# Value products on 16-bit operands in a kernel of two expert layers and one attention

## What is computed

```python
x = x + 0.5 * ffn(layernorm(x))
x = x + attention(layernorm(x))
x = x + 0.5 * ffn(layernorm(x))

def attention(x):                      # per sequence and head
    q, k, v = x @ (codes * repeat(scales, 32)) + b     # 256 -> 16 heads of 128
    attn = softmax(q @ k.T / sqrt(128))                # 512 x 512
    return (attn @ v) @ Wo + bo

def ffn(x):                            # router picks 2 of 16 experts
    return shared(x) + sum over the 2 of weight * expert(x)
```

## Time and profile before

| | us |
|---|---|
| median of 3 runs | 1041.41 (1041.18 to 1042.96) |
| the profiled execution | 1044.5 |
| its span, first to last instruction | 1042.7 |

### The profile page before, as it was taken

How to read it: one execution, slowest core, us unless ns; L and a number is a source line. 1 busy time by engine, 2 the same in 40 slices (tenths; PEclk the granted TensorE clock), 3 DMA queues, 4 the chain that set the end, 5 groups by cost and what they waited for, 6 DMA issues and landing times. The chain is left out here.

```text
span 1042.7 us, 18753 instructions
## 1 busy us (share of the span) xinstructions
PE 973.6 (93%) x5314; PEld 839.2 (80%) x5314; DVE 799.0 (77%) x1682; ACT 676.0 (65%) x1485; POOL 625.7 (60%) x916
## 2 busy tenths in 40 slices
PE   5669999899999999999999999999999999888996
PEld 4559987677888888888888888888888887668995
DVE  7777567889887787777877777787878888567766
ACT  4635644767687677677777776777776776325662
POOL 1740448776346768577788577687745456861155
PEclk9779999999999999999999999999999999789999
DMA  8867652775545764877768878767765447997755
GB/s 306 315 249 242 209 182 71 157 157 109 99 82 127 150 134 90 173 197 162 184 131 187 213 192 177 193 145 153 192 132 101 82 81 172 259 387 251 233 170 177
DMA packets 329891, 183.07 MB, mean 176 GB/s; under 512 B 273344, under 2 KB 314944, under 8 KB 329152
## 3 DMA queue, kind: packets, MB, share of 16 engines
q1 hardware_dynamic: 323056, 155.66, 60.5%
q0 software_dynamic: 6432, 20.98, 6.0%
q10 hardware_dynamic: 304, 5.24, 1.4%
HBM read 73.31 MB, written 46.92 MB: 115 GB/s over the span
## 5 line engine op out<-in xcount | busy, mean ns | idle before, releaser
L682 POOL CAST R<-turned 128x512 fp32r<-128x512 f16 x512 | 289.7, 615 | 212.9 <-DMA turned<-work 148.7
L1722 PE MATMUL bank<-R 128*128 128x512 f32 (+2 forms) x1056 | 388.4, 368 | 16.9 <-DVE R L1360 5.9
L1723 PE MATMUL bank<-R 128*128 128x512 f32 (+2 forms) x1056 | 377.8, 358 | 0.0
L1724 PE MATMUL bank<-R 128*128 128x512 f32 (+2 forms) x1056 | 377.3, 357 | 0.0
L1722 PEld LDWEIGHTS bank<-R 128*128 128x128 f32 x1056 | 202.7, 192 | 50.7 <-issue 9.8
L1724 PEld LDWEIGHTS bank<-R 128*128 128x128 f32 x1056 | 202.6, 192 | 28.3
L1723 PEld LDWEIGHTS bank<-R 128*128 128x128 f32 x1056 | 203.1, 192 | 27.0
L992 ACT ACTIVATE bank<-bank,soft 128x512 f32<-128x512 f32 x256 | 170.3, 667 | 70.5 <-DVE soft L1532 70.5
L1525 DVE SCALAR_TENSOR_TENSOR R<-bank,bias,R 128x512 fp32r<-128x512 f32 x192 | 143.8, 749 | 64.4 <-ACT R L1012 38.1
L1532 DVE TENSOR_REDUCE soft<-bank 128x1 f32<-128x512 f32 x256 | 168.6, 686 | 25.0 <-PE bank L1724 25.0
L1546 DVE SCALAR_TENSOR_TENSOR work<-bank,soft,work 128x512 f16<-128x512 f32 x256 | 185.3, 743 | 0.8 <-ACT work L1005 0.8
(11 more groups left out here) (164 smaller groups left out, 1379.1 us busy)
## 6 DMA issues: line engine op xcount, KB each, us to landing
work<-in_parts SPq DMA_DIRECT2D x64, 256.0 KB, 3.6
work<-in_ffn_w SPq DMA_DIRECT2D x34, 384.0 KB, 4.7
work<-xs_dram SPq DMA_DIRECT2D x96, 128.0 KB, 2.4
y_tiles<-work SPq DMA_DIRECT2D x48, 256.0 KB, 2.9
w_dram<-work SPq DMA_DIRECT2D x16, 768.0 KB, 4.5
R<-w_dram SPq DMA_DIRECT2D x16, 768.0 KB, 9.7
y_tiles<-in_empty ACTq DMA_DIRECT2D x2, 2176.0 KB
X<-in_x SPq DMA_DIRECT2D x4, 512.0 KB, 5.1
```

Source lines behind the costliest of these rows:

```text
L682: nc.gpsimd.tensor_copy(whole_into(m, l, kb), whole_block(m, u, l, kb)).then_inc(s["cast_pool"], 1)
L1722: nc.tensor.matmul(out, ah, bh, start=(i == 0 and first), stop=False)
L1723: nc.tensor.matmul(out, ah, bl, start=False, stop=False)
L1724: last = nc.tensor.matmul(out, al, bh, start=False, stop=(i == n - 1))
```

## The change

- The value products read the turned fp16 planes themselves, as four blocks of 128 columns each. Values V are fp16 planes, hi and lo. The casts and PT are gone; POOL only waits for the transposes. `pv` waits for both transposes ahead of its first product; `flip` and the shared weights' load wait for the value products (o) where they waited for casts.
- So that the values fit fp16, a group's value weights and bias are multiplied by a power of two, alpha. POOL squares the scaled weights of the four heads and adds them up (`squared`, `fold`), sends the 128 sums to HBM and reads them back on all partitions (`sums_out`, `sums_in`), adds them (`total`). DVE makes alpha and its inverse with five short integer operations (`scale_of`). POOL multiplies the weights with it (`halved`), `y_add` multiplies by the inverse. For groups 1 to 3 this is cut into six steps in as many units (`VALUE_STEPS`: from unit 4, 21 and 37, steps at +0, +1, +2, +3, +5, +6, DVE at +4); for group 0 it stands in the first feed-forward block.
- PT's room is put ahead of the value weights. Nine experts (0 to 8) are loaded during the attention (units 30, 31, 41, 45, 46, 52, 60, 61, 62), seven behind it.

```diff
+UP = 127 + 11 + 63
+DOWN = 254 - UP - 15
...
+FREE = 8192
...
+             nc.sbuf_tensor("V", [P, 2, 2, QB, HG * HD], F16) as m.V, \
...
-        m.PT = c.cut(2 * QB * S).rearrange("p (l b n) -> p l b n", l=2, b=QB)
...
+def value_start(g):
+    return 4 if g == 1 else HG * B * g - 11
...
+EXPERT_AT = {30: 0, 31: 1, 41: 2, 45: 3, 46: 4, 52: 5, 60: 6, 61: 7, 62: 8}
+VALUE_STEPS = {value_start(g) + step: (g, step) for g in range(1, NG) for step in (0, 1, 2, 3, 5, 6)}
+SCALED = {value_start(g) + 4: g for g in range(1, NG)}
...
-    return m.turned[u % 2][:, :, :, l, kb, :]
+    return m.turned[u % 2][:, :, :, l, kb, :].rearrange("p h q n -> p (h q) n")
...
-        wait(sp, s["cast_pool"], 8 * (u - 1))
+        wait(sp, s["o"], u - 1)
...
+    def fold(a, n):
+        while n > 1:
+            n //= 2
+            st.link(nc.gpsimd.tensor_tensor(a[:, 0:n], a[:, 0:n], a[:, n:2 * n], ALU.add))
...
+    def squared(g, i):
+        codes = m.raw[:, 0, part_of("v", g, i) % 4, :]
+        st.link(nc.gpsimd.tensor_tensor(one_head if i else squares, codes, codes, ALU.mult))
+        if i:
+            st.link(nc.gpsimd.tensor_tensor(squares, squares, one_head, ALU.add))
+    def sums_out(g):
+        fold(squares, KT * HD)
+        nc.gpsimd.dma_start(m.peak_dram[g:g + 1, :].rearrange("a p -> p a"), squares[:, 0:1])\
...
+    def scaled_bias(g):
+        pool.wait_ge(s["alpha"], 2 * g + 2)
...
+            st.link(nc.gpsimd.tensor_scalar(codes, codes, m.alpha[:, g, 0:1], None, ALU.mult))
...
-        wait(pool, s["o"], u)
-        for kb, l in ((0, 0), (0, 1), (1, 0), (1, 1), (2, 0), (2, 1), (3, 0), (3, 1)):
-            cast(u, l, kb)
...
+    def value_step(g, step):
+        if step < 2:
+            for i in (2 * step, 2 * step + 1):
+                scaled("v", g, i)
+            for i in (2 * step, 2 * step + 1):
+                squared(g, i)
+            if step == 1:
+                sums_out(g)
+        elif step == 2:
+            sums_in(g)
+        elif step == 3:
+            total(g)
+        else:
+            if step == 5:
+                scaled_bias(g)
+            for i in (2 * step - 10, 2 * step - 9):
+                halved("v", g, i)
...
+    def scale_of(g):
+        power, unit = m.peak[:, 1:2].bitcast(I32), 2.0 ** EXPONENT
+        dve.wait_ge(s["total"], g + 1)
...
-            ins = v_.scalar_tensor_tensor(out=x2, in0=bank[6 + i][:], scalar=1.0 / P_SCALE, in1=x2,
+            ins = v_.scalar_tensor_tensor(out=x2, in0=bank[6 + i][:], scalar=m.alpha[:, it // B, 1:2], in1=x2,
...
     def pv(u, kb):
-        pe.wait_ge(s["cast_pool"], 8 * u + 2 * kb + 2)
+        if kb == 0:
+            for half in range(2):
+                pe.wait_ge(m.flipped[half], 16 * (u + 1))
...
-        ph, pl = m.PT[:, 0, kb, :], m.PT[:, 1, kb, :]
-        nc.tensor.matmul(bank[1][:], vh, ph, start=(kb == 0), stop=False)
+        ph, pl = (whole_block(m, u, l, kb) for l in range(2))
+        out = bank[1][:].rearrange("p (a n) -> p a n", a=QB)
+        nc.tensor.matmul(out, vh, ph, start=(kb == 0), stop=False)
```

More of the change, by code:

```diff
@@ L198, in build @@
         m.y_tiles = nc.dram_tensor("y_tiles", (NR * P, D), F32, kind="Internal").ap()
+        m.peak_dram = nc.dram_tensor("peak_dram", (NG, P), F32, kind="Internal").ap()
         m.sh_dram = nc.dram_tensor("sh_dram", (P, 2 * W_SH), F32, kind="Internal").ap()
@@ L241, in build @@
         m.begin, m.shift, m.own, m.skipped = c.cut(SEG + 1), c.cut(SEG), c.cut(NE), c.cut(QB)
+        m.alpha = m.own[:, 0:2 * NG].rearrange("p (g n) -> p g n", g=NG)
         assert CH <= 4 * D
@@ L404, in weight_work @@
         for hh in range(HG):
-            at = 4 + hh // 2 if g == 1 else first - 8 + hh // 2
+            at = value_start(g) + hh // 2
             work.setdefault(at, []).append(("v", g, hh))
@@ L556, in sync_program @@
             empty_spare()
[L557 to L571, removed]
+        if u in EXPERT_AT:
+            e = EXPERT_AT[u]
+            sp.wait_ge(s["pre_out"], 16 * (e + 1))
+            if e >= 5:
+                sp.wait_ge(s["v"], 48 if e == 5 else 64)
+            if e == 8:
+                sp.wait_ge(s["o"], UNITS - 4)
+            expert(e)
+    sp.wait_ge(s["o"], UNITS - 1)
     sp.dma_start(m.sh_words, m.sh_dram).then_inc(s["sh_in"], 16)
@@ L574, in sync_program @@
     sp.wait_ge(s["q"], UNITS)
-    sp.wait_ge(s["y"], UNITS - 3)
-    expert(8)
     sp.wait_ge(s["s"], 4 * UNITS)
+    expert(15)
+    sp.wait_ge(s["y"], UNITS - 2)
+    expert(11)
+    sp.wait_ge(s["y"], UNITS - 1)
     expert(12)
-    sp.wait_ge(s["y"], UNITS - 2)
+    sp.wait_ge(s["o"], UNITS)
     expert(9)
[L581 to L584, removed]
     expert(10)
     sp.wait_ge(s["y"], UNITS)
-    expert(11)
+    expert(13)
+    expert(14)
     tile_loads(1)
@@ L708, in pool_program @@
         fetch(0, 0, j)
-    for value in values:
-        scaled(*value)
+        if j == 3:
+            scaled(*values[0])
+            scaled(*values[1])
+        if j == 4:
+            squared(0, 0)
+            squared(0, 1)
+        if j == 5:
+            scaled(*values[2])
+            scaled(*values[3])
+        if j == 6:
+            squared(0, 2)
+            squared(0, 3)
+        if j == 7:
+            sums_out(0)
+    sums_in(0)
+    total(0)
+    scaled_bias(0)
     pool.wait_ge(s["r_dn"], NPAIR)
@@ L759, in pool_program @@
     for t in range(1, UNITS + 1):
-        casts(t - 1)
-        for part in WEIGHTS_AT.get(t, ()):
-            weights(*part)
+        turned(t - 1)
+        if t in VALUE_STEPS:
+            value_step(*VALUE_STEPS[t])
+        for kind, g, hh in WEIGHTS_AT.get(t, ()):
+            if kind != "v":
+                weights(kind, g, hh)
         if t == 1:
```

48 lines of the change are left out of this document (36 added, 12 removed).

## The result

| | us |
|---|---|
| predicted | 1031.0 (1026 to 1039) |
| the changed kernel, median of 4 runs | 1053.24 (1050.48 to 1059.51) |
| the kernel before, beside it, median of 4 | 1041.30 (1040.94 to 1042.96) |
| ratio, 95% interval | 1.0121 (1.0094 to 1.0148) |
| the profiled execution, its span | 1059.51, 1057.7 |

A forecast was written before the change was run, and what follows sets the result against it. PE was taken to bound the attention, without a gap. Value products 7.6 plus late casts 3.0 made 10.6 us off the median 1041.4: 1030.8, rounded 1031.0, range 1026 to 1039 with (a) and (c), (b) left out.

The forecast's parts named there:

- What bounds the kernel, and reading it by starts: Attention, 290 to 860 us: PE busy 567.90 of 570.00 us, no gap by product starts, 10.98 us a head.
- Value products, 7.6 us: Attention's 768 value products: 16-bit operands save 10.8 ns each, counted for 708 of them, 7.6 us.
- lower bound: Value products: 8.3 ns saved each, 5.9 us, if a 16-bit product costs 5.0 ns over its columns.
- Rival (a): Value products: weight load already hidden, 13.3 ns belong to the product's issue; only the casts' 3.0 us left, 1038.4; chance 0.14.
- (b): Value products: four blocks of 128 each restart the stream, 39.8 ns more a product, 1069 us; chance 0.09.
- Late casts, 3.0 us: Attention: PE runs behind POOL's casts in five heads, 3.6 us; half of the second head's given back, 3.0 us.
- The new wait on both transposes, 0: Ahead of each head's first value product: planes ready at least 2.1 us before PE wants them, cost 0.
- POOL's new work in the attention, 0: Attention: worst head at most 11.8 us of POOL work, below the 14.7 allowed; cost 0, cover 2.9 us.
- Group 0's exchange: Ahead of the attention: no term; one clause, DVE's first operations fall where it is idle for 4.5 us.
- ScalarE, VectorE, the moved expert loads, the end: Attention and end: each costs 0; a moved load delays the next transposes about 1.6 us, which is covered.
- (c): Transposes late behind moved expert loads or POOL's long head: four places, 2 us each, 8 us, 1039; chance 0.11.
- (d): PE's clock: a fall to half clock after waits for DVE, spared or added, 2 us either way; no chance given.

The follow-up runs named there:

- constant_scale: Changed kernel with constant scale 64, put on where ScalarE and VectorE write the value planes; no search, exchange or multiply: ratio 0.9862 to the kernel before.
- before_again: The kernel before, unchanged, traced again on the second set's chip: one run, 1045.2 us, span 1043.4.
- work_only: Changed kernel with POOL's squares, folds and sums kept, but no write or read of the sums, total constant 512: ratio 0.9940 to the kernel before.
- scale_only: Changed kernel with one edit, scale put on at the values' planes instead of by POOL's multiply on the weights: ratio 1.0062 to the kernel before.
- at_eviction_b: The kernel of at_eviction measured again, on the third set's chip: ratio 0.9930 to the kernel before.
- at_eviction: Changed kernel with pre-splits of heads 22 and 38 later, group 0's exchange five fetches earlier, scale put on at value planes: ratio 0.9898.
- write_each_head: constant_scale plus a 0.5 KB write by POOL in each of heads 10 to 52: ratio 1.0466, 63 us over constant_scale.

## Why the prediction was wrong, point by point

Two sums from traces. What the 16-bit products bring without any search for a scale (`constant_scale` against `before_again`, spans 1029.4 and 1043.4); and what the search costs as the change places it (its span of 1057.7 against 1029.4; other sets, but the kernels before differ by 0.2%). Each column rests on one trace of each kernel. By the ratios of all runs the two are 14.4 and 27 us, so the sums hold; a single row can be off by 2 or 3 us (the two traces of the kernel before differ by 2.9 in their first value product):

| us | products alone | the search, as placed |
|---|---|---|
| up to the first value product | -2.5 | +10.4 |
| 62 heads at 0.10 | -6.2 | |
| other periods | -4.5 | +3.9 (4, 5), +5.6 (22, 23), +6.7 (38, 39), +0.5 (rest) |
| from head 62's first value product on | -0.8 | +1.2 |
| sum | -14.0 | +28.3 |

**What bounds the kernel, and reading it by starts: right.**

**Value products, 7.6 us: mechanism right, size at its lower bound.** 8.3 ns a product instead of 10.8, 6.2 us over 62 heads. Their weights' load fell from 193 ns to 100. The group by form in the changed kernel:

```profile
L2062 PEld LDWEIGHTS bank<-turned,V 128*128 128x128 f16 x256 | 25.6, 100 | 24.1 <-issue 2.5
```

The Trainium skill, "TensorE: Matmul & The Clock Gate", "Wait — 56ns, not 53.3ns?", gives N/2.4 + 2.5 ns, by which 512 columns are estimated at 215.8; the trace agrees inside the row (216.0). So my 10.8 ns was right for a product inside the row. What made the term smaller is the row's first step (0.227 us, nothing saved) and, more, the ten score products behind the row, which start 0.231 us apart instead of 0.227; their cause is open. That the sum came out at the 8.3 ns of my lower bound is chance, since that bound had another reason. Rival (a) is out (0.216, not 0.227), and so is (b): four blocks of 128 cost nothing.

**Late casts, 3.0 us: undersized.** Outside the products the kernel without casts gains 7.8 us. "The first head's products wait for q" is true of the trace that I read (2.18 us for VectorE's q, at 194.00), but not of every execution: in `before_again` they wait 3.92 us for the casts, at 196.94. Against that one they start 2.5 us earlier without casts and head 0 is 0.9 shorter; against the other the start gains nothing, so these 2.5 us are the least certain. The last two heads bring 2.0 us instead of 0.8, of which the second block behind them gives 0.8 back, and head 4 brings 0.87 that I had not seen.

**The new wait on both transposes, 0: right.** It costs nothing unless the transposes are late.

**POOL's new work in the attention, 0: right for the work, wrong for the DMA in it.** This is the step that failed most. The work took 10.9 us (447.67 to 458.59) for my 11.8. "POOL starts when the planes land" was wrong (it starts when the parts land), but `work_only` shows that the work still costs nothing. What I priced at "a DMA issue of 0.96" was the 0.5 KB write: I costed its issue on POOL and not what it does to the transfers around it. That is 12.3 us at heads 22 and 38, and 3.0 to 3.6 at head 4 when it falls badly.

**Group 0's exchange: a step never priced.** This is the second step that failed. The prediction weighed POOL's new work against the casts that go, and in front there are none; it gave group 0 one clause, on VectorE, and the exchange there no term. VectorE's five operations are as short as I said (0.15 us each). By the runs, the multiply with the halving's wait for it costs 6.2 us (`scale_only`), the late exchange 3.1 (`at_eviction_b` against `scale_only`), and 1.3 is what `at_eviction` still has over `constant_scale`; each is a difference between two traces. `work_only`, with the multiply and no transfer, puts the multiply at 5.0 (199.45 against `constant_scale`'s 194.43, across sets), so it is the largest part either way.

**ScalarE, VectorE, the moved expert loads, the end: 0, right.** Heads 30, 31, 41, 45, 46 and 52, each with a load, have periods of 10.88. From head 62 on the changed kernel takes 144.4 us and `before_again` 144.0.

**The rivals.** (c) was the right kind, with late transposes at two of the true places, but by the wrong mechanism, at a third of the price (2 us a place), and I gave it 0.11. No rival priced the front. (d) is seen: behind the waits of 3.0 to 4.2 us at heads 4 and 22 the value products start 0.427 us apart, which is half clock, and it makes the periods behind heads 22 and 38 1.3 and 1.4 us longer than 10.88.

## What to carry over

A step that sends a DMA has two prices, its engine's time and what it does to the transfers it meets; the second was the larger here, for half a kilobyte, and only runs with the work and the transfer apart could tell them. Price the first use of a new step by itself, in its own stage, and ask which engine's queue it stands in: a factor that could be put on where a result is written anyway cost 5 to 6 us in front of DMA issues. A real gain (14 us) can be hidden under twice as much loss; measure the change without its overhead before giving it up. And one trace shows one execution: what the first value product waits for differed between two of the same kernel.

## What was not expected of the hardware

- The write of 0.5 KB, 4 bytes from each of 128 partitions (16 packets of 32 bytes in the trace), took 6.9 to 9.9 us to land, and 7.2 to 11.5 in `write_each_head`; where all its completions were recorded, the 16 came one by one over 2.3 to 7.1 us. At head 4 its packets moved from 259.6 to 260.0, 2.7 us behind the issue, and the completions followed until 265.3. The Trainium skill, "DMA: Bandwidth & Descriptors", "Anatomy of one DMA — SWDGE (gpsimd) path", gives a fixed and nearly constant cost of about 2 us, mostly completion. The completion is the long part here too, but it is neither 2 us nor constant; the measurement decides.
- Such a write holds up the other transfers under way: transposes 6.6 instead of 4.3 us, a 256 KB load 8.9 instead of 3.6. The same page, "Rules for kernel authors", says that a transpose next to ordinary DMAs needs nothing; that stands beside a rule against wrong results, and in time these runs show a price. Whether the small pieces or the completions make it was not tried with another shape of write.
- Products of 512 columns behind one another start after 216.0 ns with 16-bit operands and after 226.7 with fp32r ones, weight loads of 100 and 193 ns beside them.
